# A routed mixture-of-experts round: the next tile is transposed two chunks sooner, its token numbers copied one round sooner

## The chip, the cores and the metric

The kernel runs on one core of a Trainium2 chip. The metric is the device time of one execution in microseconds (us). The engines are TensorE (PE; its weight loads are shown as PEld), VectorE (DVE), ScalarE (ACT), GpSimd (POOL) and SyncE (SP), which work side by side and wait for one another by semaphores. Transfers are issued by SP (direct ones, hardware queue) and by POOL (indirect ones with row numbers, software queue).

## What is computed

The reference is one block of gated cross-attention and one gated feed-forward block with two experts, on 8 x 256 tokens of 256 numbers, in float32. The part that the change touches is the second one, cut here to what matters:

```python
gate_scores = xf @ gate_w.T
top1 = jnp.argmax(gate_probs, axis=-1)
one_hot = jax.nn.one_hot(top1, N_ROUTING, dtype=xf.dtype)
masked = xf[None, :, :] * one_hot.T[:, :, None]
h = jax.nn.relu(jnp.einsum('end,edh->enh', masked, w1) + b1[:, None, :])
expert_out = jnp.einsum('enh,ehd->end', h, w2) + b2[:, None, :]
routing_output = expert_out.sum(axis=0)
shared = jax.nn.relu(xf @ sw1 + sb1) @ sw2 + sb2
return (routing_output + shared).reshape(B, S, D)
```

Every token thus gets a shared part, the part of its own expert (256 to 1024 hidden to 256), and for the other expert a constant row, since its input there is zero.

## The kernel before

**Stages.** Up to about 227 us the core works through attention and the shared part of the feed-forward block. Meanwhile each token's normalised row is scattered into `sorted_dram`, expert 0 from one end and expert 1 from the other, each row with its token number as a last column. The shared results lie in `part_dram`. Then come the routed rounds: 8 rounds of `RTOK` = 256 sorted rows, numbered 0 to 7 here, and behind them a half round for the 128 rows in which the experts meet. Each engine runs them in two loops, one per expert (`routed(j, e)`, loop variable `j`); in this run the first loop holds the earlier rounds and the second the later ones.

**Precision.** Each float32 operand is cut in two fp32r parts, hi and lo, and each product is three matmuls (`cut`). So ACT writes a hi part and the unrounded value, and DVE subtracts the two for the lo part.

**One round.** HIDDEN = 1024 is worked in 8 chunks of 128 (`HC`). I call the six matmuls that make chunk n's hidden values H_n (into `h_ps` or `s_ps`) and the six that add its share to the result Y_n (into `y_ps`). PE's order is H0 H1 H2 H3 Y0 H4 Y1 H5 Y2 H6 T Y3 H7 Y4 Y5 Y6 Y7: T is `sorted_turn(j + 1)`, four transposes of the next tile `xs` into one PSUM bank. ACT does for each chunk `hT_hi` and `h32` (lines 1083 and 1086), and behind chunk 6 `sorted_hi(j + 1)`, which copies the bank out (line 1018). DVE does for each chunk `hT_lo` (line 1469), which lets Y_n start, and besides:

- behind chunk 0, `gather_token` from the last column of `xs` (line 1475), once the tile has landed and the gathers of the round before are in; it raises `ids_copied`
- behind chunk 5, `scatter_token` from `gather_token` (line 1481), once the scatters of the round before have landed (`rows_out`)
- behind chunk 6, `sorted_lo(j + 1)` (line 1402), which needs `sorted_hi`
- behind Y7, `final` (line 1488), from `y_ps` and `part`; Y0 of the next round waits for it.

**Transfers of a round.** There is one buffer `xs`. SP loads the tile of round j + 1 into it once T of that buffer's last tile is done (`xsT_ps`) and its token numbers are out (`ids_copied`), and in rounds 0 to 3 it then copies a quarter of one expert's weights, 1 MB, into `sw` for the half round:

```python
def routed(j):
    sp.wait_ge(xsT_ps, j + 1)
    sp.wait_ge(ids_copied, j + 1)
    load_sorted(j + 1 - again)
```

POOL waits for `ids_copied` of the round and for `final` of the round before, issues two gathers from `part_dram` into `part` (line 807), waits for them, adds the other expert's row (line 814), and after `final` issues two scatters to `out` (line 821).

**What comes just ahead of round 0.** SP stores the last shared results (line 545), reads four numbers of the plan from SBUF into registers (lines 576 to 579), enters its loop and only then issues the load of tile 1. Tile 0 was loaded and transposed earlier, from the written-out orders.

Of the kernel before, what the change touches and what calls it, by code (L numbers as in the profile page):

```python
# [14 lines left out]
BATCHES, SEQ, DIM = 8, 256, 256  # L15
# [37 lines left out]
ROW = DIM + 1  # L53
# [23 lines left out]
LO_ON_POOL = (1, 4, 5)  # L77
FOLDED = {2, 4, 11, 12, 16, 19, 25, 29, 30, 31}
SORTED_BANK = 0
PE_ORDER = """  # L80
    warm.0 yt.0 yt.1 yt.2 yt.3 vt warm.1 kp.0.0 in.0.0 kp.0.1 kp.1.0 qy.0.1 kp.1.1 sc.0.0 vp.0 in.1.0 vp.1 vp.2
    qy.1.1 vp.3 sc.0.1 sc.0.2 sc.0.3 sc.1.0 sc.1.1 tn.0.0.0 tn.0.1.1 in.2.0 qy.2.1 sc.1.2 sc.1.3 tn.0.2.0
# [80 lines left out]
def build(nc, x, ctx_768, g_xattn, g_ffn, wq, bq, wk, bk, wv, bv, wo, bo,  # L163
# [13 lines left out]
    with ctx:  # L177
# [82 lines left out]
        xs = sb("xs", [P, RT, ROW])  # L260
# [587 lines left out]
        def _(act):  # L848
# [240 lines left out]
            def routed(j, e):  # L1089
                for c in range(HC):  # L1090
                    hidden(j, c, e)
                    if c == 6:
                        sorted_hi(j + 1, SORTED_BANK)

            with act.Fori(0, first) as j:
# [20 lines left out]
        def _(dve):  # L1116
# [282 lines left out]
            def sorted_lo(j, m):  # L1399

                dve.wait_ge(xsT_hi, j + 1)
                nc.vector.tensor_tensor(xsT[1][:, bass.ds(j % 2, 1), :, :].rearrange("p o k s -> p (o k s)"),
                                        bank[m][:, :],
                                        xsT[0][:, bass.ds(j % 2, 1), :, :].rearrange("p o k s -> p (o k s)"),
                                        ALU.subtract).then_inc(xsT_lo, 1)
# [4 lines left out]
            for step, at in walk(DVE_ORDER):  # L1410
# [47 lines left out]
                if step == "xsl":  # L1458
                    sorted_lo(0, *at)

            dve.wait_ge(seam_rdy, 1)
            first = dve.value_load(plan_int[0:1, FIRST:FIRST + 1], min_val=1, max_val=RTILES)
            rounds = dve.value_load(plan_int[0:1, ROUNDS:ROUNDS + 1], min_val=RTILES, max_val=MOST_ROUNDS)

            def routed(j, e):
                q = CHUNKS_SHARED + j * HC
                for c in range(HC):
                    dve.wait_ge(h_32, q + c + 1)
                    nc.vector.tensor_tensor(hT[1][:, c % HB, 0:RTOK], h32[:, c % 2, 0:RTOK], hT[0][:, c % HB, 0:RTOK],  # L1469
                                            ALU.subtract).then_inc(h_lo, 1)  # L1470
                    if c == 0:

                        dve.wait_ge(xs_in, 16 * (j + 1))
                        dve.wait_ge(gathered, 32 * j)
                        nc.vector.tensor_copy(gather_token[:, :], xs[:, :, DIM:ROW].rearrange("p t o -> p (t o)")
                                              ).then_inc(ids_copied, 1)
                    if c == 5:

                        dve.wait_ge(ids_copied, j + 1)
                        dve.wait_ge(rows_out, 32 * j)  # L1480
                        nc.vector.tensor_copy(scatter_token[:, :], gather_token[:, :]).then_inc(scatter_ids, 1)
                    if c == 6:
                        sorted_lo(j + 1, SORTED_BANK)

                dve.wait_ge(y_used, CHUNKS_SHARED + (j + 1) * HC)
                dve.wait_ge(part_rdy, RT * (j + 1))
                dve.wait_ge(rows_out, 32 * j)
                nc.vector.scalar_tensor_tensor(  # L1488
                    out=final[:, :, :].rearrange("p t d -> p (t d)"),
                    in0=y_ps[:, 0:RT, :].rearrange("p t d -> p (t d)"), scalar=gains[:, 1:2],  # L1490
                    in1=part[:, :, :].rearrange("p t d -> p (t d)"), op0=ALU.mult, op1=ALU.add
                ).then_inc(final_rdy, 1)
# [40 lines left out]
        def _(pe):  # L1533
# [293 lines left out]
            def routed(j, e):  # L1827
                q = CHUNKS_SHARED + j * HC
                pe.wait_ge(xsT_lo, j + 1)
                for n in range(HC + 3):  # L1830
                    if n < HC:

                        pe.wait_ge(h_32, q + n - 3)
                        for kc in range(KC):
                            ins = cut(hidden_bank(n % 4)[:, 0:RTOK],
                                      lambda m: ew1_sb[e][m][:, kc, n * P:(n + 1) * P],
                                      lambda m: xsT[m][:, bass.ds(j % 2, 1), kc, :].rearrange("p o s -> p (o s)"),
                                      kc == 0, kc == KC - 1)
                        ins.then_inc(h_in_ps, 1)
                    if n == 6:  # L1840
                        sorted_turn(j + 1, SORTED_BANK)
                    if n >= 3:
                        c = n - 3
                        pe.wait_ge(h_lo, LO_DVE + j * HC + c + 1)
                        if c == 0:
                            pe.wait_ge(y_out, len(UNITS))
                            pe.wait_ge(final_rdy, j)
                        for t in range(RT):
                            ins = cut(y_ps[:, t, :], lambda m: hT[m][:, c % HB, t * P:(t + 1) * P],
                                      lambda m: ew2_sb[e][m][:, c, :], c == 0 and t == 0, c == HC - 1,  # L1850
                                      skip_group_check=True)
                        ins.then_inc(y_used, 1)
# [51 lines left out]
```

## Time and profile before

| | us |
|---|---|
| median of 3 runs | 337.58 |
| lowest and highest | 336.97, 338.42 |
| span of the profiled execution | 339.1 |
| round 0 starts, half round starts (in the span) | 227.37, 325.42 |

The profile is one execution; its times count from the start of its span. A row of a timeline gives start, length, engine, line, operation, written and read tiles and a count of instructions in a row, and in brackets how long the engine was idle ahead of it and who ended that. The ends of matmuls are modelled, so their starts are the firmer numbers.

### The profile page before, as it was taken

To read this page: it belongs to the slowest core of one execution; us is meant where nothing else is said; L and a number is where in the kernel's file an instruction comes from. 1 tells how busy PE (TensorE), PEld (TensorE's weight loads), DVE (VectorE), ACT (ScalarE), POOL (GpSimd) and SP (SyncE) were. 2 spreads that over 40 slices of the span, in tenths; PEclk is the share of its full clock that TensorE was granted. 3 is DMA by queue.
4 is the path that set the end of the run, shared out by engine and by line. 5 is a ranking of instruction groups with operands and counts; after the bars stand their busy time and mean duration, and the time that the engine had idled before them with its cause. 6 is when DMAs were issued, how large, how long until landed. Compare 5 with 4: busy or idle time off the path is not lost.

```text
span 339.1 us, 7286 instructions
## 1 busy us (share of the span) xinstructions
PE 318.2 (94%) x2363; PEld 282.2 (83%) x2363; DVE 227.9 (67%) x516; ACT 215.6 (64%) x483; POOL 184.0 (54%) x261
## 2 busy tenths in 40 slices
PE   6997879899999999999999999999999999999993
PEld 5764666678988877788799889999999999999992
DVE  6999689999878899796767675534333544353463
ACT  2855898976786665658957584547546546464652
POOL 8226979885652564757371177432255536534542
PEclk9998599999999999999999999999999999999997
DMA  7992855274422030053160100315246233212300
GB/s 191 299 340 38 241 126 160 42 198 128 109 80 56 2 97 29 0 139 121 15 240 2 62 2 31 127 32 188 79 168 217 66 151 93 77 35 75 92 32 28
DMA packets 38150, 35.68 MB, mean 105 GB/s; under 512 B 16608, under 2 KB 35060, under 8 KB 37613
## 3 DMA queue, kind: packets, MB, share of 16 engines
q1 hardware_dynamic: 34568, 27.36, 28.5%
q0 software_dynamic: 2720, 7.32, 6.4%
q10 hardware_dynamic: 837, 0.67, 0.8%
q8 instruction: 14, 0.23, 0.3%
q14 instruction: 11, 0.09, 0.1%
HBM read 21.20 MB, written 9.85 MB: 92 GB/s over the span
## 4 chain that ended last, share of the span: by engine, by line
PE 61%; DVE 15%; ACT 8%; issue 7%; DMA 5%; POOL 1%; POOLq 1%; SPq 1%; DVEq 0%; ACTq 0%
PE y_ps L1535 20%; PE h_ps L1535 17%; PE bank L1535 9%; PE s_ps L1535 9%; DMA x_all<-in_x 5%; PE bank L1668 4%; ACT probs L947 2%; DVE rsum L1264 2%; DVE smax L1246 1%; DVE probs L1258 1%; DVE stats L1147 1%; DVE other_sum L1232 1%; ACT pT L956 1%; DVE hT_lo L1469 1%; ACT xn L898 1%
## 5 line engine op out<-in xcount | busy, mean ns | idle before, releaser
L690 POOL TENSOR_TENSOR probs<-probs,rinv 128x616 f32<-128x616 f32 x32 | 39.1, 1223 | 37.8 <-DVE rinv L1268 37.5
L1535 PE MATMUL y_ps<-sw,hT_hi 128*128 128x256 f32 x272 | 57.1, 290 | 1.2 <-DVE hT_lo L1513 1.2
L1535 PE MATMUL y_ps<-ew,hT_hi 128*128 128x256 f32 x256 | 54.1, 286 | 1.8 <-DVE hT_lo L1469 1.7
L1469 DVE TENSOR_TENSOR hT_lo<-h,hT_hi 128x256 fp32r<-128x256 f32 x64 | 29.2, 457 | 38.5 <-ACT h L1086 35.2
L1535 PEld LDWEIGHTS y_ps<-sw,hT_hi 128*128 128x128 f32 x272 | 44.9, 191 | 2.9 <-DVE hT_lo L1513 1.8
L1535 PEld LDWEIGHTS y_ps<-ew,hT_hi 128*128 128x128 f32 x256 | 42.4, 188 | 3.0 <-DVE hT_lo L1469 3.0
L1535 PE MATMUL h_ps<-x2T_hi,sw 128*128 128x512 f32 (+1 forms) x160 | 43.6, 359 | 0.1
L1083 ACT ACTIVATE hT_hi<-h_ps,vec_cols 128x256 fp32r<-128x256 f32 x32 | 15.2, 475 | 39.5 <-PE h_ps L1535 35.3
L995 ACT ACTIVATE hT_hi<-h_ps,vec_cols 128x512 fp32r<-128x512 f32 (+1 forms) x40 | 24.6, 614 | 21.9 <-PE h_ps L1535 17.3
L1535 PE MATMUL y_ps<-sw,hT_lo 128*128 128x256 f32 x136 | 38.4, 282 | 0.0
L1535 PE MATMUL y_ps<-ew,hT_lo 128*128 128x256 f32 x128 | 35.9, 280 | 0.0
L1264 DVE TENSOR_REDUCE rsum<-probs 128x8 f32<-128x616 f32 x32 | 25.1, 785 | 9.3 <-ACT probs L947 5.9
L821 POOL DMA_INDIRECT out<-final,scatter_token x16 | 18.0, 1127 | 24.6 <-DVE final L1488 19.2
L1535 PEld LDWEIGHTS h_ps<-x2T_hi,sw 128*128 128x128 f32 x160 | 26.8, 190 | 3.5 <-issue 0.8
L716 POOL TENSOR_TENSOR hT_lo<-h,hT_hi 128x512 fp32r<-128x512 f32 (+1 forms) x15 | 17.2, 1151 | 21.9 <-ACT h L1000 21.7
L1535 PE MATMUL h_ps<-x2T_lo,sw 128*128 128x512 f32 (+1 forms) x80 | 27.8, 348 | 0.0
L956 ACT ACTIVATE pT<-bank 128x512 f32<-128x512 f32 x40 | 23.7, 611 | 5.9 <-PE bank L1668 5.4
L1535 PE MATMUL h_ps<-xsT_parts,ew 128*128 x192 | 26.5, 280 | 0.0
L1535 PE MATMUL s_ps<-xsT_parts,ew 128*128 x192 | 26.4, 279 | 0.0
L1379 DVE TENSOR_TENSOR hT_lo<-h,hT_hi 128x512 fp32r<-128x512 f32 (+1 forms) x25 | 16.2, 654 | 15.0 <-ACT h L1000 15.0
L1535 PEld LDWEIGHTS y_ps<-sw,hT_lo 128*128 128x128 f32 x136 | 26.0, 191 | 0.2
L1668 PE MATMUL bank<-ident,probs 128*128 128x128 f32 (+1 forms) x160 | 24.3, 284 | 1.4 <-ACT pT L956 1.0
(206 smaller groups left out, 837.1 us busy)
## 6 DMA issues: line engine op xcount, KB each, us to landing
v_diag<-v_rows SPq DMA_DIRECT2D x16, 256.0 KB
stage<-in_L_ffn_w SPq DMA_DIRECT2D x4, 1024.0 KB, 5.6
sw<-ew SPq DMA_DIRECT2D x4, 1024.0 KB
xs<-sorted_dram SPq DMA_DIRECT2D x8, 257.0 KB
stage<-in_L_ffn_sw SPq DMA_DIRECT2D x2, 1024.0 KB, 6.6
x_all<-in_x SPq DMA_DIRECT2D x1, 1536.0 KB, 9.8
part_dram<-x_all SPq DMA_DIRECT2D x3, 512.0 KB, 2.9
k_dram<-probs SPq DMA_DIRECT2D x2, 616.0 KB, 5.9
```

The lines of the kernel that those rows point to most:

```text
L690: nc.gpsimd.tensor_tensor(pq, pq, rinv[:, b % 2, k, :].unsqueeze(2).to_broadcast([P, HG, KEYS]), ALU.mult).then_inc(p_ready, 1)
L716: nc.gpsimd.tensor_tensor(hT[1][:, q % HB, 0:width], h32[:, q % 2, 0:width], hT[0][:, q % HB, 0:width], ALU.subtract).then_inc(h_lo_pool, 1)
L821: pool.indirect_dma_start(out=out[:, :], out_offset=bass.IndirectOffsetOnAxis(ap=scatter_token[:, t:t + 1], axis=0), in_=final[:, t, :], i ...
L947: ins = nc.scalar.activation(to[:, h * KEYS:(h + 1) * KEYS], score_banks(quarter)[:, h // HH, keys], ACT.Exp, bias=smax[:, b % 2, k, h:h + 1])
L956: nc.scalar.activation(pT[:, 2 * u:2 * u + 2, :].rearrange("p c s -> p (c s)"), bank[m][:, :], ACT.Copy).then_inc(pT_sb, 1)
L995: nc.scalar.activation(hT[0][:, q % HB, 0:width], h_ps[:, q % 2, 0:width], ACT.Relu, bias=b1_sb[:, 0, c:c + 1]).then_inc(h_hi, 1)
L1083: nc.scalar.activation(hT[0][:, c % HB, 0:RTOK], hidden_bank(c % 4)[:, 0:RTOK], ACT.Relu, bias=b1_sb[:, 1 + e, c:c + 1]).then_inc(h_hi, 1)
L1264: nc.vector.tensor_reduce(out=rsum[:, b % 2, k, :], in_=probs[:, b % 2, k, :].rearrange("p (h k) -> p h k", k=KEYS), axis=AX_X, op=ALU.add ...
L1379: nc.vector.tensor_tensor(hT[1][:, q % HB, 0:width], h32[:, q % 2, 0:width], hT[0][:, q % HB, 0:width], ALU.subtract).then_inc(h_lo, 1)
L1469: nc.vector.tensor_tensor(hT[1][:, c % HB, 0:RTOK], h32[:, c % 2, 0:RTOK], hT[0][:, c % HB, 0:RTOK], ALU.subtract).then_inc(h_lo, 1)
L1535: return nc.tensor.matmul(out_, lhsT, rhs, start=start, stop=stop, **kw)
L1668: ins = nc.tensor.transpose(bank[m][0:ROWS[c], v * SEQ + t * P:v * SEQ + (t + 1) * P], probs[:, b % 2, g * TB + t, ROW0[c]:ROW0[c] + ROWS[ ...
```

## The change

T moves from behind H6 to behind H4 on PE, and with it `sorted_hi` on ACT and `sorted_lo` on DVE, from behind chunk 6 to behind chunk 4. The copy of the token numbers moves from behind chunk 0 of their own round to behind chunk 6 of the round before; the first copy stands ahead of DVE's loops. The count on `gathered` for which this copy waits grows by one round with it: it is now the gathers of the round in which it stands.

```diff
+TURN_AT = 4
@@ ACT
                 for c in range(HC):
                     hidden(j, c, e)
-                    if c == 6:
+                    if c == TURN_AT:
                         sorted_hi(j + 1, SORTED_BANK)
@@ DVE, ahead of the loops
+            def token_ids(j):
+
+                dve.wait_ge(xs_in, 16 * (j + 1))
+                dve.wait_ge(gathered, 32 * j)
+                nc.vector.tensor_copy(gather_token[:, :], xs[:, :, DIM:ROW].rearrange("p t o -> p (t o)")
+                                      ).then_inc(ids_copied, 1)
+
+            dve.wait_ge(xs_in, 16)
+            nc.vector.tensor_copy(gather_token[:, :], xs[:, :, DIM:ROW].rearrange("p t o -> p (t o)")
+                                  ).then_inc(ids_copied, 1)
@@ DVE, in a round
-                    if c == 0:
-
-                        dve.wait_ge(xs_in, 16 * (j + 1))
-                        dve.wait_ge(gathered, 32 * j)
-                        nc.vector.tensor_copy(gather_token[:, :], xs[:, :, DIM:ROW].rearrange("p t o -> p (t o)")
-                                              ).then_inc(ids_copied, 1)
+                    if c == TURN_AT:
+                        sorted_lo(j + 1, SORTED_BANK)
                     if c == 5:
 
                         dve.wait_ge(ids_copied, j + 1)
                         dve.wait_ge(rows_out, 32 * j)
                         nc.vector.tensor_copy(scatter_token[:, :], gather_token[:, :]).then_inc(scatter_ids, 1)
                     if c == 6:
-                        sorted_lo(j + 1, SORTED_BANK)
+                        dve.wait_ge(scatter_ids, j + 1)
+                        token_ids(j + 1)
@@ PE
-                    if n == 6:
+                    if n == TURN_AT:
                         sorted_turn(j + 1, SORTED_BANK)
```

On PE, in the first loop, the transposes before. They stand behind H6 (into `s_ps`), and the row after them is the start of Y3:

```order
L1535 MATMUL s_ps<-xsT_parts,ew 128x256 [waits h_32]
L1535 MATMUL s_ps<-xsT_parts,ew 128x256 x5
L1769 ISA
L1772 MATMUL bank<-ident,xs 128x128 [waits xs_in]
L1772 MATMUL bank<-ident,xs 128x128 x3
L1844 REGISTER_ALU
L1535 MATMUL y_ps<-ew,hT_hi 128x256 [waits h_lo]
```

And now, behind H4 (into `h_ps`) and ahead of Y1:

```order
L1543 MATMUL h_ps<-xsT_parts,ew 128x256 [waits h_32]
L1543 MATMUL h_ps<-xsT_parts,ew 128x256 x5
L1777 ISA
L1780 MATMUL bank<-ident,xs 128x128 [waits xs_in]
L1780 MATMUL bank<-ident,xs 128x128 x3
L1852 REGISTER_ALU
L1543 MATMUL y_ps<-ew,hT_hi 128x256 [waits h_lo]
```

What moved is the wait for `xs_in`: it now stands ahead of Y1, H5, Y2 and H6 too.

On DVE, in the first loop, the end of a round before, from the lo part of chunk 5 to that of chunk 7:

```order
L1469 TENSOR_TENSOR hT_lo<-h,hT_hi 128x256 [waits h_32]
L1481 COPY scatter_token<-gather_token 128x2 [waits rows_out,ids_copied]
L1468 REGISTER_ALU
L1469 TENSOR_TENSOR hT_lo<-h,hT_hi 128x256 [waits h_32]
L1401 REGISTER_ALU
L1402 ISA [waits xsT_hi]
L1402 REGISTER_ALU
L1402 TENSOR_TENSOR xsT_parts<-bank,xsT_parts 128x512
L1468 REGISTER_ALU
L1469 TENSOR_TENSOR hT_lo<-h,hT_hi 128x256 [waits h_32]
```

And now:

```order
L1480 TENSOR_TENSOR hT_lo<-h,hT_hi 128x256 [waits h_32]
L1487 REGISTER_ALU [waits ids_copied]
L1488 COPY scatter_token<-gather_token 128x2 [waits rows_out]
L1479 REGISTER_ALU
L1480 TENSOR_TENSOR hT_lo<-h,hT_hi 128x256 [waits h_32]
L1464 REGISTER_ALU [waits scatter_ids]
L1465 REGISTER_ALU [waits xs_in]
L1466 CAST gather_token<-xs 128x2 [waits gathered]
L1479 REGISTER_ALU
L1480 TENSOR_TENSOR hT_lo<-h,hT_hi 128x256 [waits h_32]
```

Between the lo parts of chunks 6 and 7 the subtraction of 128x512 is gone, and the small copy with its wait for `gathered` has come.

## Rows read from the trace of the kernel before

**Rows 1.** The page: busy time of the engines, and the group of DVE's lo parts.
```profile
PE 318.2 (94%) x2363; PEld 282.2 (83%) x2363; DVE 227.9 (67%) x516; ACT 215.6 (64%) x483; POOL 184.0 (54%) x261
...
L1469 DVE TENSOR_TENSOR hT_lo<-h,hT_hi 128x256 fp32r<-128x256 f32 x64 | 29.2, 457 | 38.5 <-ACT h L1086 35.2
```
**Rows 2.** Timeline of PE, H0 and H1 of rounds 0 to 4, 6 and 7, and of the half round.
```profile
227.37 1.56 PE L1535 MATMUL h_ps<-xsT_parts,ew 128*128 x12
...
239.68 1.58 PE L1535 MATMUL h_ps<-xsT_parts,ew 128*128 x12
...
252.85 1.64 PE L1535 MATMUL h_ps<-xsT_parts,ew 128*128 x12
...
265.51 1.58 PE L1535 MATMUL h_ps<-xsT_parts,ew 128*128 x12
...
277.57 1.58 PE L1535 MATMUL h_ps<-xsT_parts,ew 128*128 x12
...
301.09 1.59 PE L1535 MATMUL h_ps<-xsT_parts,ew 128*128 x12
...
313.63 1.60 PE L1535 MATMUL h_ps<-xsT_parts,ew 128*128 x12
...
325.42 1.11 PE L1535 MATMUL h_ps<-xsT_parts,sw 128*128 x8
```
**Rows 3.** Who waited for whom, 222 to 339.1 us: total, times, longest us.
```profile
DVE final L1488 <- POOL part L814: 4.8, 2, 3.5
...
DVE scatter_token L1481 <- DMA out<-final,scatter_token: 3.2, 2, 2.8
PEld y_ps L1535 <- DVE hT_lo L1469: 3.0, 6, 0.8
```
**Rows 4.** Timelines of SP (store, load, weight copy, load) and DVE (first token numbers).
```profile
228.35 0.36 SPq L545 DMA_DIRECT2D part_dram<-x_all  x1
232.01 0.42 SPq L549 DMA_DIRECT2D xs<-sorted_dram  x1
232.78 0.63 SPq L592 DMA_DIRECT2D sw<-ew  x1
243.29 0.39 SPq L549 DMA_DIRECT2D xs<-sorted_dram  x1
...
229.67 0.16 DVE L1475 CAST gather_token<-xs 128x2 uint32<-128x2 f32 x1
```
**Rows 5.** Timeline of PE in round 0: H4, start of Y1, H6, T.
```profile
230.88 0.86 PE L1535 MATMUL h_ps<-xsT_parts,ew 128*128 x6
231.58 0.28 PE L1535 MATMUL y_ps<-ew,hT_hi 128*128 128x256 f32 x1
...
233.70 0.86 PE L1535 MATMUL s_ps<-xsT_parts,ew 128*128 x6
234.93 0.66 PE L1772 MATMUL bank<-ident,xs 128*128 128x128 f32 x4 [0.37 <-DMA xs<-sorted_dram]
```
**Rows 6.** Timeline of PE and windows of PE (last: granted clock, DMA) at 28 to 44 us.
```profile
38.80 0.55 PE L1535 MATMUL bank<-xnT_hi,wqo_hi 128*128 128x256 f32 x1 [1.65 <-DVE xnT_lo L1239]
...
28.00:31.80 3.80, 1.95 (x7) 1.00 0.20 31
31.80:42.00 10.20, 7.96 (x38) 0.50 0.73 193
42.00:44.00 2.00, 1.94 (x20) 0.99 0.95 211
```
**Rows 7.** Timeline of POOL: the adds behind the gathers of rounds 0 and 3.
```profile
240.40 1.42 POOL L814 TENSOR_TENSOR part<-part,other_row 128x256 f32<-128x256 f32 x2 [4.97 <-DMA part<-part_dram,gather_token]
...
275.68 1.61 POOL L814 TENSOR_TENSOR part<-part,other_row 128x256 f32<-128x256 f32 x2 [2.88 <-DMA part<-part_dram,gather_token]
```
**Rows 8.** Timeline of DVE at the end of round 3: `sorted_lo`, then the lo part of chunk 7.
```profile
275.23 0.69 DVE L1402 TENSOR_TENSOR xsT_parts<-bank,xsT_parts 128x512 f32 x1 [0.23 <-ACT xsT_parts L1018]
275.84 0.86 DVE L1469 TENSOR_TENSOR hT_lo<-h,hT_hi 128x256 fp32r<-128x256 f32 x1
```

## The prediction, made before the changed kernel was run

> **What bounds the kernel now.** I read the page first: PE is busy 94% of the span [rows 1], so time can come only from the few places where PE stands still. In the routed rounds these are found by taking the starts of the rounds one from the next [rows 2]. Round 0 takes 239.68 - 227.37 = 12.31 us, round 1 13.17, round 2 12.66, round 3 12.06, rounds 4 and 5 together 301.09 - 277.57 = 23.52, or 11.76 each, round 6 12.54 and round 7 11.79. Every round has the same 96 matmuls and one T, so 11.76 is what PE needs for a round, and the rest is waiting: 0.55, 1.41, 0.90, 0.30, 0, 0, 0.78 and 0.03 us, together 3.97 us. That is all the change could ever win here.
>
> The waits by name [rows 3] say what it is, of the rounds and what lies around them. DVE copies `scatter_token` only when the scatters of the round before have landed, once 2.8 us late (round 1). The lo parts hold up PE's weight loads six times, 3.0 us in all. One example is round 3, where `sorted_lo` runs at 275.23 and the lo part of chunk 7 behind it, at 275.84, ends at 276.70 [rows 8]; Y7 would have been ready for it at about 276.4. `final` waited for POOL's adds 3.5 us in round 0, because the first gathers landed only at 240.40 [rows 7]. And T of round 0 waited 0.37 us for the load of tile 1 [rows 5].
>
> **Part 1: T behind H4, in rounds 1 to 7.** PE's work is only reordered: no instruction more. T needs tile j + 1 in `xs`, 2 x (H + Y) sooner than now. Its load is issued when `ids_copied` is raised, which also moves, from chunk 0 of the round to chunk 6 of the one before, some 3 us, so from round 1 on the load is in well before T: in round 1 the copy of the numbers can come as soon as the gathers of round 0 are in, 240.40, the load starts near 240.7 instead of 243.29 [rows 4], and T comes after 246. Price nothing. The cover is these 3 us; were it gone, T would wait in every round.
>
> What it wins: `sorted_lo`, 0.69 us, no longer stands between the lo parts of chunks 6 and 7, and on ACT `sorted_hi` no longer stands ahead of chunk 7. The rounds in which chunk 7's lo part was late are 2, 3 and 6: 0.90 + 0.30 + 0.78 = 1.98 us. Bounds are nothing and 1.98. What is late next is the new wait between the same two lo parts: `gather_token` needs the gathers of its own round. In round 3 they are in at 275.68 [rows 7], which is 10.17 us after the round's start at 265.51. With the small copy [rows 4], a lo part [rows 1] and some 0.1 us between them, 0.16 + 0.46 + 0.1, chunk 7 is ready at about 10.9; Y7's turn is at 11.76 - 0.71 = 11.05. So it fits, with 0.15 us to spare. I take -1.8 us, nearly all, because this landing is a late one, 2.88 us of waiting: in this round the 1 MB copy into `sw` is in flight with the gathers, and the copy now starts some 3 us sooner with the load ahead of it.
>
> **Part 2: T behind H4, in round 0.** This is the place where the change costs. The load of tile 1 is issued at 232.01, and not because of `ids_copied`: SP stores at 228.35 and then needs 3.7 us for the reads of its four registers and the entry of its loop [rows 4]; its wait on the numbers, which were out at 229.67 + 0.16 = 229.83, cost nothing. Copying the numbers sooner therefore does not bring this load forward. It lands in time for T at 234.93 [rows 5]. PE has done H4 by 231.58, when Y1 starts now. T will stand there, and PE with it, for 234.93 - 231.58 = 3.35 us. Now T follows H6, which would let it start at 233.70 + 0.71 = 234.41, so 0.52 of this is paid already. Round 0 gets longer by 3.35 - 0.52 = **2.83 us**; everything behind T in the round (Y1, H5, Y2, H6 and the rest) is queued behind it.
>
> **Part 3: round 1 hides what it waited for.** When PE arrives 2.83 us later, the things it waited for in round 1 are there: `final` of round 0 depends on the adds after 240.40, which do not move, and the scatters of round 0, whose landing held up `scatter_token`, start at most 1 us later than before. I let all of round 1's 1.41 us go: **-1.41**. The bound on the other side is nothing (the scatters move with PE). The new wait for `gathered` in round 0 ends at 240.40, and chunk 7's lo part would then be done at 241.1; in the new order Y7's turn comes at 242.51 - 0.71 = 241.8, so this hides too, with 0.7 us to spare.
>
> **Part 4: the clock.** PE has no standstill of 3.35 us anywhere in the trace; the longest is the 1.65 us ahead of 38.80. But the granted clock fell from 2.4 to 1.2 GHz (1.00 to 0.50) at 31.8, at the end of 3.8 us in which PE was busy for only 1.95 [rows 6]. The standstill in round 0 is emptier than that: 3.35 us of nothing. I expect the clock to fall there. It was back at 42.0, 3.2 us after the last gap's end at 38.80. In round 0 PE works without a gap behind T, so I take 3.2 us at half speed, which costs half of it, **+1.6 us**. The bounds: nothing, if the clock holds, and the whole 10.2 us from 31.8 to 42.0 at half, +5.1 us.
>
> The Trainium skill bears on this ("TensorE: Matmul & The Clock Gate", Part 1): the half rate is the default, and "activity releases the throttle". By that rule a PE that works densely behind the gap gets its clock back soon, and the sum would be near mine and not near +5.1; the trace shows the return only once, after a gap inside the slow stretch.
>
> **The sum.** +2.83 - 1.41 - 1.8 + 1.6 = +1.2 us. Against the profiled execution it is 339.1 + 1.2 = 340.3. That execution lies 1.5 us over the median of the runs, 337.58; the difference should carry over, so I forecast **338.8 us**, a little slower. Less than 0.5%, 1.7 us, is about what a measurement of this kernel can't tell from no change.
>
> The small copy ahead of the loops, 0.16 us on DVE, lies in its wait for the first `h32` of round 0; without that cover it would be 0.2 us. The half round's load comes sooner and nothing there waits for it.
>
> **Rivals.**
>
> *The clock holds.* For it: the gap is a single one, with dense work on both sides, and the fall in the trace came after two gaps. Then +2.83 - 1.41 - 1.8 = -0.4: 337.2 us.
>
> *The clock stays down longer*, up to the stretch of [rows 6]. Between +1.2 and 1.2 - 1.6 + 5.1 = +4.7; middle 340.5, slower. Against it: PE there had gaps inside the stretch.
>
> *The gather wait decides.* DVE stands in front of `gathered` between the lo parts of chunks 6 and 7, with chunk 7's lo part, and so Y7, behind it. It decides from the point where gathers land more than 10.3 us after the round's start. Round 3 has 10.17, and 4.97 us of waiting for the first gathers shows how late they can be when the weight copy goes ahead of them. If they land 0.6 us later in seven rounds, that is 7 x 0.4 = +2.8 on top: 341.6.
>
> *The late lo parts have another cause* than `sorted_lo` (ACT itself is late there), and rounds 2, 3 and 6 keep their waits: +1.2 + 1.8 = +3.0, 340.6.
>
> *The load is not late in round 0.* If SP did wait for the numbers after all and issued at 229 to 230, T would find its tile, only the wins would be left, about -1.8 and round 0's gather wait: 336.0 us. Against it stands the 3.7 us between SP's two issues.
>
> **How the numbers follow.** Chances: forecast 0.47, clock holds 0.24, clock down longer 0.12, gather wait 0.07, other cause of late lo parts 0.05, load not late 0.05. The range from 336.6 to 341.0 takes in the first two with their bounds on parts 1 and 3, and the middle of the next. Faster by over 0.5% (under 335.9) needs the last case or the second with luck: 0.08. Slower by over 0.5% (over 339.3): the three slower rivals and the upper fifth or so of the forecast, 0.33. Within: 0.59.
>
> **What the changed profile would show.** Part 2: T of round 0 with an idle time of about 3.3 us ahead of it, ended by the load of `xs`, and SP's load still 3.7 us behind its store. Part 4: a stretch of 0.50 in the granted clock between 235 and 240. Part 3: no wait of 2.8 us for `scatter_token` with PE behind it, round 1 at 11.8. Part 1: rounds 2 to 7 all near 11.8, and no PE wait on lo parts. I would be wrong if T of round 0 does not wait, or if the rows of waits name `gather_token` behind the gathers with PE idle after it.

## The result, and the profile after

| | kernel before | changed kernel |
|---|---|---|
| median | 337.62 us (22 runs) | 341.48 us (22 runs) |
| ratio, with its 95% interval | | 1.0106 [1.0079, 1.0134] |
| span of the profiled execution | 339.1 us | 340.7 us |
| time of the profiled execution | about 340.9 us | 342.54 us |
| rounds 0 to 7, start to start of the half round | 98.05 us | 99.98 us |
| what they take over 8 x 11.76 (waits, and the slow clock where it falls) | 3.97 us | 5.90 us |

The change makes the kernel 1.1% slower, 3.9 us by the medians and 3.6 by the ratio. The forecast was 338.8, in a range up to 341.0, so it missed. (One of the 22 runs, at 441.64 us, was disturbed and is left out of the ratio; without it the changed kernel's median is 340.97, since no run lies between 340.97 and 341.98 us.) The 340.9 of before is its span and the 1.84 us by which the changed kernel's time exceeds its span, 342.54 - 340.7.

First the starts of the routed rounds, read as in [rows 2]. The timeline of PE in the changed kernel, H0 and H1 of rounds 0, 1, 2 and 7 and the start of the half round:

```profile
227.09 1.56 PE L1543 MATMUL h_ps<-xsT_parts,ew 128*128 x12
...
244.83 1.57 PE L1543 MATMUL h_ps<-xsT_parts,ew 128*128 x12
...
256.55 1.62 PE L1543 MATMUL h_ps<-xsT_parts,ew 128*128 x12
...
315.33 1.56 PE L1543 MATMUL h_ps<-xsT_parts,ew 128*128 x12
...
327.07 1.12 PE L1543 MATMUL h_ps<-xsT_parts,sw 128*128 x8
```

Round 0 takes 244.83 - 227.09 = 17.74 us, where it took 12.31. Round 1 takes 11.72, and every later round lies between 11.72 and 11.80. So all that the change costs is in round 0, and every other round is at the floor.

In round 0 the changed kernel has T with its wait, on PE, and on SP the store, load and weight copy in the same places as in [rows 4]:

```profile
234.56 1.12 PE L1780 MATMUL bank<-ident,xs 128*128 128x128 f32 x4 [3.10 <-DMA xs<-sorted_dram]
...
228.07 0.36 SPq L546 DMA_DIRECT2D part_dram<-x_all  x1
231.74 0.42 SPq L550 DMA_DIRECT2D xs<-sorted_dram  x1
232.51 0.63 SPq L593 DMA_DIRECT2D sw<-ew  x1
```

PE stands for 3.10 us, against 0.37 in [rows 5]. SP's load is still 3.67 us behind its store, although the token numbers are now out long before. The four transposes take 1.12 us and not 0.66, which already tells of the clock. The windows of PE (start and end, length, busy time and instructions, granted clock, DMA share, GB/s), ahead of the standstill, in it, behind it, and behind that:

```profile
223.70:231.30 7.60, 7.60 (x65) 1.00 0.11 36
231.30:234.56 3.26, 0.16 (x2) 0.88 0.48 149
234.56:240.60 6.04, 6.04 (x29) 0.50 0.54 183
240.60:244.80 4.20, 4.20 (x37) 1.00 0.21 48
...
233.70:234.56 0.86, 0.00 (x0) 0.53 0.98 343
```

The granted clock is 1.00 (2.4 GHz), drops to 0.50 (1.2 GHz) before the standstill is over (0.53 already in the 0.86 us ahead of T, the last row), and stays there for 6.04 us of work in which PE has not a single gap: 29 instruction records where the same length at full clock holds some 50.

The waits, read as in [rows 3], 222 us to the end:

```profile
PEld bank L1780 <- DMA xs<-sorted_dram: 3.3, 1, 3.3
PE bank L1780 <- DMA xs<-sorted_dram: 3.1, 1, 3.1
...
PEld y_ps L1543 <- DVE hT_lo L1521: 1.8, 3, 0.8
...
DVE gather_token L1466 <- DMA part<-part_dram,gather_token: 0.2, 1, 0.2
```

`final` behind POOL's adds and `scatter_token` behind the scatters are gone from the list, and so are PE's waits for lo parts of the routed rounds; those that are left belong to the half round (line 1521). The new wait of `gather_token` is there once, with 0.2 us.

### The profile page after: what moved, and what is told of

The parts are those of the page before. It is cut to its first block, busy times and chain, and to the rows that moved or that the text cites. A ratio compares the mean times of both kernels' runs of the same rounds, so it can differ in the third digit from the quotient of the medians.

```text
span 340.7 us, 7287 instructions
## 1 busy us (share of the span) xinstructions
PE 319.1 (94%) x2363; PEld 284.0 (83%) x2363; DVE 231.1 (68%) x517; ACT 216.2 (63%) x483; POOL 182.9 (54%) x261
## 4 chain that ended last, share of the span: by engine, by line
PE 67%; DVE 13%; ACT 7%; DMA 5%; issue 4%; SPq 1%; POOL 1%; ACTq 0%; DVEq 0%; POOLq 0%
PE y_ps L1543 25%; PE h_ps L1543 18%; PE s_ps L1543 9%; PE bank L1543 8%; DMA x_all<-in_x 5%; PE bank L1676 4%; ACT probs L948 2%; DVE rsum L1265 2%; DVE smax L1247 1%; PE bank L1780 1%; ACT pT L957 1%; DVE probs L1259 1%; DVE stats L1148 1%; DVE other_sum L1233 1%; ACT xn L899 1%
## 5 line engine op out<-in xcount | busy, mean ns | idle before, releaser
L1480 DVE TENSOR_TENSOR hT_lo<-h,hT_hi 128x256 fp32r<-128x256 f32 x64 | 30.3, 473 | 37.6 <-ACT h L1087 37.6
L1543 PEld LDWEIGHTS y_ps<-ew,hT_hi 128*128 128x128 f32 x256 | 43.2, 193 | 0.0
```

What stands on the lines that cost most here:

```text
L1543: return nc.tensor.matmul(out_, lhsT, rhs, start=start, stop=stop, **kw)
```

## The experiments

Their names: a "standstill" is PE's idle time ahead of T in round 0. "Half speed" is a granted clock of 0.50. The round lengths are all read as above.

**How much of the waiting in [rows 2] is the kernel's own?** The kernel before, unaltered, was profiled a second time.

> The kernel before, unchanged, for a second profile. Theory: the profiled execution on which the prediction was built was a slow one (its span 339.1 would be a time of about 340.9, against a median of 337.6), and the waits of 3.97 us in its rounds were partly its own. Then another execution near the median shows well under 2 us of waiting over the eight rounds, that is 94.1 us plus less than 2. Rival: the waits are the same 3.97 us in every execution and the difference to the median lies ahead of the routed rounds; then the rounds again take 98 us.

Measured: 337.42 us, 1.0006 [0.9976, 1.0036], span 335.5, time of this execution 337.30. PE's timeline, H0 and H1 of rounds 0, 1 and 2 and the half round:

```profile
225.91 1.56 PE L1535 MATMUL h_ps<-xsT_parts,ew 128*128 x12
...
237.93 1.58 PE L1535 MATMUL h_ps<-xsT_parts,ew 128*128 x12
...
251.14 1.59 PE L1535 MATMUL h_ps<-xsT_parts,ew 128*128 x12
...
321.89 1.12 PE L1535 MATMUL h_ps<-xsT_parts,sw 128*128 x8
```

The rounds take 95.98 us, so their waits are 1.90 us and not 3.97. By round: 0.26, 1.45, 0.12, 0.13, and nothing from there on. Round 1's wait is the same in both executions. The waits of rounds 2, 3 and 6, which were 0.90, 0.30 and 0.78, are 0.12, 0.13 and 0.01. They belonged to that one execution. The traces show where they came from there. The first row is the start of Y1 in round 2 of the execution of [rows 2], so H4 was done at 257.13; then ACT's `hT_hi` of chunk 4 in that round, of chunk 5 in round 3 and of chunk 4 in round 6, and last that of chunk 4 in round 2 of the second execution:

```profile
257.13 0.28 PE L1535 MATMUL y_ps<-ew,hT_hi 128*128 128x256 f32 x1
...
258.62 0.47 ACT L1083 ACTIVATE hT_hi<-h_ps,vec_cols 128x256 fp32r<-128x256 f32 x1 [1.69 <-PE h_ps L1535]
...
272.75 0.47 ACT L1083 ACTIVATE hT_hi<-h_ps,vec_cols 128x256 fp32r<-128x256 f32 x1 [1.97 <-PE s_ps L1535]
...
307.36 0.47 ACT L1083 ACTIVATE hT_hi<-h_ps,vec_cols 128x256 fp32r<-128x256 f32 x1 [2.23 <-PE h_ps L1535]
...
255.58 0.47 ACT L1083 ACTIVATE hT_hi<-h_ps,vec_cols 128x256 fp32r<-128x256 f32 x1 [0.41 <-PE h_ps L1535]
```

ACT began chunk 4 of round 2 1.5 us after H4 was done, where the second execution needs 0.2 us (H4 done at 255.38), and every lo part behind it came late. In the first execution ACT was late like this in each of rounds 2 to 7 (in 4, 5 and 7 without holding PE up), in the second in none. Why ACT was late is not shown.

Round 0 starts 1.46 us sooner in the second execution, 225.91 against 227.37. The stretch of half speed of [rows 6], 10.2 us there, is 3.4 us long here:

```profile
37.70:41.10 3.40, 3.40 (x16) 0.50 1.04 305
```

**Is the late load the cause?** SP's register reads go ahead of its last store, in the changed kernel (twice) and in the kernel before (twice).

```diff
@@ SP
                 if step == "ps":
+                    if at[0] == len(UNITS) - 1:
+                        sp.wait_ge(seam_rdy, 1)
+                        sp.wait_ge(filled, 16)
+                        rounds = sp.value_load(plan_int[0:1, ROUNDS:ROUNDS + 1], min_val=RTILES, max_val=MOST_ROUNDS)
...
                     store_part(*at)
@@ behind the stages
-            sp.wait_ge(seam_rdy, 1)
-            sp.wait_ge(filled, 16)
-            rounds = sp.value_load(plan_int[0:1, ROUNDS:ROUNDS + 1], min_val=RTILES, max_val=MOST_ROUNDS)
...
```

The other three reads, shown as "...", move with the first.

> The changed kernel, but SP reads its four registers ahead of its last store and not behind it, so that the load of tile 1 is issued right behind the store (about 228.5 instead of 231.74) and lands before H4 is done. Theory (standstill plus clock in round 0 are the whole loss): the 3.1 us of standstill and the 2.8 us of half clock go, and 5.9 us less than the changed kernel would be 335.6; but PE then reaches the end of round 0 before the first gathers are in (240.8), so I expect 1 to 1.5 us of waiting for the copy of the token numbers and 336.5 to 337.5 us, a ratio to before of 0.997 to 1.001. Rival (the new order costs something in every round): the rounds stay longer than 11.76 us and the time stays at 340 or more.

> The kernel before with SP's register reads ahead of its last store, as in e1. It tells whether the new order is worth anything once its standstill is gone. Theory: the weight copy of round 0 is out of the way of the first gathers here too, so the waits of rounds 0 and 1 shrink, and what is left for the new order is only the late lo parts, under 0.5 us: 336 to 337 us, ratio 0.994 to 0.999, and within 0.3% of e1. Rival (the early transposes are worth the 2 us that the prediction gave them): e1 is over 1.5 us faster than this.

> The changed kernel with SP's four register reads ahead of its last store, a second time, beside the kernel before with the same edit. In their profiles both had no waits left in the routed rounds (sums 0.26 and -0.11 us), so by the theory that the change has nothing more to win once the load of tile 1 is early, both have the same time within 0.3%, near 336 to 337, ratio 0.994 to 0.998. Rival: the new order itself costs something that the profiled execution didn't show (T's wait in round 0 with the load 1.4 us after the store): then this one is slower than its twin by 1 to 1.5 us, at ratio 0.998 to 1.000.

> The kernel before with SP's four register reads ahead of its last store, a second time and on the same chip as its twin with the change. If the first look (335.88, ratio 0.993) holds: ratio 0.991 to 0.996, and no PE wait over 0.3 us in rounds 0 to 7. If that look owed something to its chip, the ratio is 0.997 to 1.000.

| | first time | second time, both on one chip |
|---|---|---|
| changed kernel | 337.33, 0.9985 [0.9954, 1.0017] | 336.90, 0.9992 [0.9962, 1.0023] |
| kernel before | 335.88, 0.9931 [0.9896, 0.9966] | 336.54, 0.9974 [0.9949, 1.0000] |

The changed kernel with this edit, on SP and PE:

```profile
228.41 0.37 SPq L546 DMA_DIRECT2D part_dram<-x_all  x1
229.38 0.41 SPq L550 DMA_DIRECT2D xs<-sorted_dram  x1
...
232.02 0.66 PE L1780 MATMUL bank<-ident,xs 128*128 128x128 f32 x4 [0.22 <-DMA xs<-sorted_dram]
```

The load comes 0.97 us behind the store instead of 3.67, the standstill is 0.22 us (0.41 the second time), round 0 takes 12.14 us, and the time falls by 4.2 us against the changed kernel's first median. The edit brings two transfers forward, the load and the weight copy behind it, and with the copy early the first gathers land sooner too (last section). So the whole loss hangs on what SP issues late ahead of round 0; the standstill by itself is tested at the end. The edit is also the version to keep, without the change. The kernel before with it (second time), H0 of round 0 and of the half round:

```profile
226.27 1.56 PE L1535 MATMUL h_ps<-xsT_parts,ew 128*128 x12
...
320.24 1.11 PE L1535 MATMUL h_ps<-xsT_parts,sw 128*128 x8
```

Eight rounds in 93.97 us are 11.75 each, no wait at all. It was 0.7% faster in one comparison and 0.3% in the other, whose interval just reaches 1. The second set was run on another chip to see whether the first owed something to its chip, and leaves that open. With the edit the new order has nothing left to win, and by the second pair, 336.90 and 336.54, little to lose (rounds of 94.80 and 93.97 us in the profiled executions).

**T alone, in all rounds.** T behind H4; the token numbers copied behind chunk 0, as before. The edit stands on ACT and DVE, and as `n == 4` on PE.

```diff
-                    if c == 6:
+                    if c == 4:
                         sorted_hi(j + 1, SORTED_BANK)
```

> One half of the change alone: T stands behind H4, but the token numbers are copied behind chunk 0 of their own round, as before. By the prediction's step on the cover: the next tile's load is issued about 3.6 us after a round's start (before: 243.29 - 239.68), a load took 2.9 us to its end there (232.01 to 234.93), so the tile is in 6.5 us after the start, while T's turn comes 4.2 us after it (231.58 - 227.37). If the sooner copy is what covers T, T waits some 2 us in each of rounds 1 to 7, less where DVE's copy comes early in the round, and the rounds have 12.5 to 14 us: 8 to 14 us over before, ratio 1.02 to 1.04. The rival, that PE's move alone made no wait except in round 0 and the sooner copy is needless: rounds 1 to 7 at 11.8, time as the changed kernel's, 341.5, ratio 1.010. Round 0 should show the same 3.1 us standstill either way, since its load is late behind SP's register reads.

Measured: 350.05 us (4 runs), 1.036 [1.0294, 1.0426]. PE's timeline, T of rounds 0, 1 and 2 and H0 of round 2, and SP's load in round 2:

```profile
234.30 0.66 PE L1772 MATMUL bank<-ident,xs 128*128 128x128 f32 x4 [3.23 <-DMA xs<-sorted_dram]
...
249.05 0.66 PE L1772 MATMUL bank<-ident,xs 128*128 128x128 f32 x4 [1.30 <-DMA xs<-sorted_dram]
...
262.31 0.66 PE L1772 MATMUL bank<-ident,xs 128*128 128x128 f32 x4 [1.34 <-DMA xs<-sorted_dram]
...
256.60 1.57 PE L1535 MATMUL h_ps<-xsT_parts,ew 128*128 x12
...
259.23 0.40 SPq L549 DMA_DIRECT2D xs<-sorted_dram  x1
```

T waits in all eight rounds. In rounds 1 to 6 it is 1.2 to 1.34 us, less than the 2 us that I had expected, since the load is issued 2.63 us behind the round's start at 256.60 and not 3.6. The prediction's cover is real: without the sooner copy the move costs in every round.

**The token numbers alone.** The changed kernel with `TURN_AT = 6`.

> The changed kernel with the transposes back behind the seventh chunk: the half of the change that copies the token numbers out a round sooner, alone. Theory: no standstill in round 0 beyond some 0.3 us, no fall of the clock; the copy waits in round 0 for the first gathers (about 240.6), which puts about 1 us on PE in place of the wait before final; rounds 1 to 7 at 11.8 or a little more. 337.5 to 338.8 us, ratio 1.000 to 1.004. Rival (the wait for the gathers between the lo parts of chunks 6 and 7 is what costs): 340 or more, with PE waits on lo parts in several rounds.

Measured: 341.55 us (6 runs), 1.0119 [1.0071, 1.0166], as slow as the whole change. That is the time of the expectation's rival, but with a wait in round 0 only. PE with its longest idle time, DVE just before it, and the windows of PE around it:

```profile
241.68 0.58 PE L1543 MATMUL y_ps<-ew,hT_hi 128*128 128x256 f32 x1 [2.19 <-DVE hT_lo L1480]
...
240.58 0.17 DVE L1466 CAST gather_token<-xs 128x2 uint32<-128x2 f32 x1 [2.79 <-DMA part<-part_dram,gather_token]
240.68 0.95 DVE L1480 TENSOR_TENSOR hT_lo<-h,hT_hi 128x256 fp32r<-128x256 f32 x1
...
239.50:241.60 2.10, 0.00 (x0) 1.00 0.00 0
241.60:245.00 3.40, 3.32 (x15) 0.51 0.86 287
245.00:250.00 5.00, 5.00 (x44) 0.99 0.40 142
```

This is the prediction's rival "the gather wait decides", in round 0 alone. DVE stands for 2.79 us in front of `gathered`, with chunk 7's lo part behind it, and PE 2.19 us in front of Y7. Round 0 takes 15.22 us. Then the clock falls here too, for 3.4 us. Not all of the 4.1 us is this: the rounds of this execution take 98.32 us, 2.3 more than in the second execution of the kernel before, and another 2.0 us lie ahead of round 0, which starts at 227.91, though PE's work there is unchanged. In the whole change the wait for the gathers is hidden by the standstill ahead of it, and PE pays for the first wait that it meets.

**Where T stands in round 0.** Once `TURN_AT = 5` in all rounds, and once 6 in round 0 and 4 in all others (round 0 written out ahead of the loops of PE, ACT and DVE).

```diff
+            routed(0, 0, FIRST_TURN_AT)
-            with pe.Fori(0, first) as j:
+            with pe.Fori(1, first) as j:
                 routed(j, 0)
```

> The changed kernel with TURN_AT = 5, T behind H5, one H and one Y later than in the change. Theory: the standstill in round 0 is 1.41 us shorter, about 1.7 us. If the clock holds at that, round 0 takes 13.2 to 13.7 us and the time is 338 to 339; if it falls, about 1.7 us more, 340. Either way the round's length is 11.76 plus the standstill plus what the clock takes. Rival (order of the later rounds costs): the same 341.5 as the change.

> The changed kernel with round 0 written out ahead of the loops, and in round 0 alone the transposes behind the seventh chunk; rounds 1 to 7 as in the change. Theory: the loss sits in round 0 only, so this gives it back: no standstill, no fall of the clock, 337 to 338.5 us, ratio 0.998 to 1.003, rounds 1 to 7 at 11.76. Rival (the order of rounds 1 to 7 costs): 340 or more.

Measured: with 5, 338.41 us, 1.0002 [0.9972, 1.0032]; with 6 in round 0, 337.03 us, 0.9994 [0.9963, 1.0025]. At 5, T waits less and the gathers take over; both idle times of PE in round 0:

```profile
233.65 0.66 PE L1780 MATMUL bank<-ident,xs 128*128 128x128 f32 x4 [1.77 <-DMA xs<-sorted_dram]
...
240.52 0.39 PE L1543 MATMUL y_ps<-ew,hT_hi 128*128 128x256 f32 x1 [1.25 <-DVE hT_lo L1480]
```

Round 0 takes 15.23 us, where 13.2 to 13.7 was expected if the clock holds: the expectation had left out the gathers. Its clock held, and all ten runs are at 339.13 us or below, above which 29 of the changed kernel's 32 lie (its two sets of runs). With 6 in round 0 the longest idle time is 0.78 us (Y7 again), rounds 0 and 1 wait 2.6 us together, and the time is that of the kernel before.

**The clock.** The changed kernel was profiled again; it was also run with round 0 written out and nothing else changed, twice; and that form with matmuls in the standstill, twice.

```diff
                     if n == turn_at:
+                        if isinstance(j, int):
+                            for _ in range(14):
+                                mm(bank[1][:, 0:P], ident[:, :], ident[:, :], True, True)
                         sorted_turn(j + 1, SORTED_BANK)
```

> The changed kernel, unaltered, to see what its standstill does to the clock in another execution and how its times are spread. Theory: the wait for tile 1 (3.1 us) is there in every execution and costs 3.4 us, and the clock falls behind it in some executions and holds in others; so the times lie in two groups, near 340 with a mean granted clock of 0.986 or more and near 343 with 0.976 to 0.982. Rival: the clock falls every time and the spread has its cause before the routed rounds; then the mean clock does not separate the two groups. Ratio 1.008 to 1.013 by both.

> The changed kernel with round 0 written out ahead of the loops and nothing else: the control for the next run. Expected as the changed kernel: T of round 0 stands 2.5 to 3.2 us, the clock falls to 0.5 for 3.4 to 7 us, rounds 1 to 7 at 11.76, 340 to 342 us. If the writing out itself matters, T waits for a clearly different time.

> The run before plus 14 matmuls of the identity with itself ahead of T in round 0, into a PSUM bank that nothing reads any more; they fill the standstill, which stays as long as it was. Theory (the standstill costs twice, once by itself and once through the clock): the clock stays at 1.00 through round 0, which gets 1.7 to 2.9 us shorter than in the control, 14.8 to 15.2 us by its length; 338 to 339.5 us. Rival (the fall of the clock is harmless, since PE then waits for others anyway): same time as the control.

> The changed kernel with round 0 written out ahead of the loops of PE, ACT and DVE and otherwise the same, as the twin of the run with the extra matmuls. Expected by the theory: a group of 3 to 6 of some 12 runs near 342 with a mean clock of 0.983 or less, the others near 339, ratio 1.005 to 1.010. By the rival the same, but with the group in the twin too.

> The written-out form with 14 matmuls of the identity into the second PSUM bank ahead of T in round 0 (work that the reference has not, its result unused), a second time. Theory (the group near 342 us is the fall of the clock behind the standstill): PE has no standstill, no run lies near 342 with a mean clock of 0.983 or less, median 338.5 to 339.5, ratio 1.003 to 1.005, and the highest group is gone. Rival (the group comes from elsewhere, such as the start or the transfers): the group stays, about as many runs as in the form without the extra work.

| | median us | ratio | round 0 | at half speed around T |
|---|---|---|---|---|
| changed kernel | 341.48 | 1.0106 [1.0079, 1.0134] | 17.74 | 6.8 |
| again | 340.50 | 1.0090 [1.0057, 1.0123] | 16.43 | 3.4 |
| written out | 339.62 | 1.0062 [1.0025, 1.0099] | 15.27 | none |
| written out, again | 341.25 | 1.0084 [1.0048, 1.0120] | 17.73 | 6.8 |
| with matmuls | 339.50 | 1.0047 [1.0015, 1.0078] | 15.18 | none |
| with matmuls, again | 338.97 | 1.0033 [1.0004, 1.0063] | 15.06 | none |

The last two columns are those of the one profiled execution of each. The same standstill, 3.01 to 3.15 us, came with 6.8 us at half speed, with 3.4 or with none. T in the written-out form, its first profile and its second (the transposes' own length tells the clock), and then the matmuls and T of the form that has them:

```profile
232.80 0.66 PE L1783 MATMUL bank<-ident,xs 128*128 128x128 f32 x4 [3.01 <-DMA xs<-sorted_dram]
...
234.10 1.11 PE L1783 MATMUL bank<-ident,xs 128*128 128x128 f32 x4 [3.03 <-DMA xs<-sorted_dram]
...
230.07 3.29 PE L1547 MATMUL bank<-ident 128*128 128x128 f32 x28
233.34 0.66 PE L1784 MATMUL bank<-ident,xs 128*128 128x128 f32 x4
```

What it costs is then plain: 17.73 - 15.27 = 2.5 us for 6.8 us at half speed, 16.43 - 15.27 = 1.2 for 3.4. The 15.27 holds about 0.3 us in which Y7 waits for chunk 7's lo part, behind the gathers, and the slow clock covers this wait in the others; so the clock by itself costs nearer 2.8 and 1.4 us.

How often it happens must be read from the runs' mean granted clocks, and these count the whole execution, the stretch of [rows 6] too. A low mean alone proves nothing of round 0: with SP's reads early, 7 of 48 runs have 0.981 or less, and six of them take 336.73 to 337.99 us; and the execution profiled in the next experiment has 3.4 us at half speed in round 0 at a mean of 0.993. So the two forms have to be compared. In the second comparison the form with a standstill has six of twelve runs at a mean of 0.981 or less, and they are its six slowest, 341.60 to 342.59 us; the other six take 338.67 to 340.90. The form with matmuls has none under 0.986 and none over 340.82. Of the 29 runs of the kernel before beside them none has 0.981 or less. In the first comparison four of ten runs against none had the low clock, though the medians, 339.62 and 339.50, hardly differ. Over both, 10 of 22 runs with a standstill have a mean of 0.982 or less, and none of 22 with the matmuls. That tells the two theories apart: a group near 342 comes from the clock, and it goes when PE works through the wait, though T starts no sooner for it.

The clock doesn't explain every long time. One run with the matmuls took 342.37 us at 0.992. The changed kernel's first set has 342.82 and 343.60 us at 0.991. In its second set the five runs at 0.982 or less (340.34 to 341.93) overlap with the other six (338.67 to 341.00). With SP's reads early (first time), where the standstill is 0.22 us, two of twelve runs took 341.10 and 341.51. Their cause is open.

What decides whether the clock falls is open too. The form alone doesn't decide it: the changed kernel showed 6.8 and 3.4 us, the written-out form none and 6.8.

**The standstill alone.** The kernel before with round 0 written out and T behind H4 in that round only.

> The kernel before with round 0 written out and T behind H4 in that round alone; everything else, the copy of the token numbers too, as before. T waits 3.0 to 3.3 us and round 0 has 15.2 us. If the step on round 1 holds, the waits of rounds 1 and 2 (1.2 to 2.3 us in the two looks at the kernel before) go, and the time is +1.5 us, or +1.5 to +4 with the clock: ratio 1.004 to 1.010, the same as the whole change. The rival, that the waits of the later rounds are independent of PE's arrival, leaves them: +3 us or more without the clock, ratio 1.010 to 1.016.

Measured: 340.68 us, 1.0085 [1.0047, 1.0123]. H0 and H1 of rounds 0, 1 and 2 on PE, and T in round 0:

```profile
225.32 1.56 PE L1539 MATMUL h_ps<-xsT_parts,ew 128*128 128x256 f32 x12
...
241.97 1.56 PE L1539 MATMUL h_ps<-xsT_parts,ew 128*128 x12
...
253.74 1.60 PE L1539 MATMUL h_ps<-xsT_parts,ew 128*128 x12
...
232.86 0.66 PE L1776 MATMUL bank<-ident,xs 128*128 128x128 f32 x4 [3.17 <-DMA xs<-sorted_dram]
```

Round 0 takes 16.65 us (3.4 us at half speed), round 1 11.77: its wait is gone with nothing changed but PE's arrival. T moved in one round of eight costs about what the whole change costs.

## Why the prediction was wrong, point by point

Parts 2 to 4 had the mechanism right; Part 4 had its size too small. What failed most is the base and, with it, Part 1. Measured against the second execution of the kernel before, whose time is that of the median, the terms are these:

| step | forecast | measured | from |
|---|---|---|---|
| Part 1, lo parts of rounds 2, 3, 6 | -1.8 | -0.3 | waits 0.12 + 0.13 + 0.01 |
| Part 2, standstill in round 0 | +2.83 | +3.25 | 15.27 - 12.02 |
| Part 3, round 1 | -1.41 | -1.49 | 13.21 to 11.72 |
| Part 4, clock, where it falls for 6.8 us | +1.6 | +2.5 | 17.73 - 15.27 |
| sum | +1.2 | +4.0 | medians: +3.9 |

That the sum meets the medians is partly luck: it holds for executions in which the clock falls for 6.8 us, and the second set of runs is 340.50 - 337.68 = 2.8 us slower than the kernel before beside it.

**The base, the step that failed first.** "That execution lies 1.5 us over the median ... the difference should carry over." It set a span against a median of times. Its own time was about 340.9, so it lay 3.3 us over the median, near the slowest of 22 runs, 341.74. A long time has its reasons. Here 2.07 us of it were the very waits that the change removes, 3.97 us where the second execution has 1.90, and 1.46 us lay ahead of round 0. Neither profiled execution of the changed kernel has these waits: rounds 1 to 7 take 82.24 and 82.31 us, and 7 x 11.76 is 82.32. The first came to 340.7, only 0.4 from the 340.3 that the sum gave. So against the execution before, in which Part 1's waits were there to be won, the sum was nearly right, with 0.28 us of luck from an earlier start of round 0. The difference to the median was what did not carry over.

**Part 1** failed with it: 0.3 us to win where it took 1.8, so the lower bound, nothing, was nearer. It blamed `sorted_lo` between the lo parts. But the second execution has `sorted_lo` in the same place and waits 0.12 and 0.13 us in rounds 2 and 3. What made rounds 2, 3 and 6 late in the execution of [rows 2] was ACT, which began chunks 4 or 5 some 1.5 to 2 us late (the rows in the first experiment). It could have been suspected, since rounds 4, 5 and 7 run the same instructions in the same order without that wait. Whether the new order would hide such lateness isn't shown, since ACT was late like this in no profiled execution of the changed kernel outside the slow clock.

**Part 2** was right in all it said: T waited 3.10 us for the load, SP's load stayed 3.67 us behind its store, and the sooner numbers did not bring it forward. The term was 0.4 short. Round 0 of the kernel before had 0.55 us of waits to give back in that execution and has 0.26 in the second, and the 15.27 holds about 0.3 us of Y7's wait behind the gathers; the standstill itself was a little shorter than forecast.

**Part 3** was right, and the standstill alone gives it by itself (round 1 in 11.77 us).

**Part 4** had the mechanism and not the size. I took 3.2 us of half speed from the last gap's end to the clock's return in [rows 6]; it was 6.8 us here, 3.4 in other executions, none in others. The Trainium skill ("TensorE: Matmul & The Clock Gate", Part 1: "activity releases the throttle") gave me the reason to take a short return. The trace agrees that the clock comes back while PE works densely, but after a time that the row of before did not show. For the price, the Trainium skill ("TensorE: Matmul & The Clock Gate", "Terms") has the penalty as the time at the lower clock times the share of the clock that is missing. That share is half here, and the estimate by it 3.4 us for 6.8. The rounds show 2.5, and the rounds decide. Two things make the difference: the half-speed stretch begins inside the standstill, where it costs nothing (0.86 us of it lie ahead of T), and it covers the 0.3 us of Y7's wait.

**The rivals.** "The clock stays down longer" is what happened in the changed kernel's first profiled execution, and it had 0.12. Its middle, 340.5, is 1.0 us short. "The gather wait decides", at 341.6, comes nearest by its number, but by luck: it was priced for seven rounds, and `gather_token` waited once, for 0.2 us, in each of the changed kernel's two profiled executions. In round 0 it stood in line behind the standstill; with the numbers alone moved it cost 2.2 us there, and in the written-out form, whose clock held, about 0.3 us in round 0 and 0.47 in round 2. So my estimate for round 0, 0.7 us to spare, did not hold either. "The clock holds" happened too, for certain in the first profiled execution of the written-out form (338.95 us). It gives 339, not the 337.2 that it was priced at from the same base. "The late lo parts have another cause", with "ACT itself is late there", had 0.05 and named the cause; what it did not see is that the lateness was that of one execution, so no round kept its wait. "The load is not late" is what the edit on SP makes true; it gives 336.9 to 337.3, against 336.0 forecast.

## What to carry to other kernels

Before a wait is counted as a gain, look whether a second execution of the same kernel has it, and set times against times: a profiled execution that lies over the median can carry waits that the median hasn't, as this one did. When an instruction that waits for a transfer is moved forward, the first pass through the loop needs its own sum, since there the transfer's issue hangs on what stands ahead of the loop; here the place of four register reads decided over 1%, and moving them in the kernel before paid 0.3 to 0.7%, more than any new order. A standstill of PE of 2 to 3 us cost its length here, and in many executions the clock's fall on top.

## What the runs showed of the hardware

- The granted clock fell to 0.50 around single standstills of 2.19 to 3.23 us with dense work on both sides, but in some executions only, for 3.4 or 6.8 us. With two idle times of 1.77 and 1.25 us in a round its profiled execution held it. With matmuls whose result is unused, 3.29 us of them in the wait, it stayed up in both profiled executions.
- Indirect gathers issued right behind a 1 MB copy landed later than those issued some 3 us after it, but by a varying amount. POOL's adds in round 0 of the changed kernel (two executions), with the copy issued 0.27 and 0.28 us ahead of the first gather, and of the same kernel with SP's reads early, where it is 3.25 us:

```profile
240.78 1.43 POOL L815 TENSOR_TENSOR part<-part,other_row 128x256 f32<-128x256 f32 x2 [5.61 <-DMA part<-part_dram,gather_token]
...
238.57 1.61 POOL L815 TENSOR_TENSOR part<-part,other_row 128x256 f32<-128x256 f32 x2 [3.34 <-DMA part<-part_dram,gather_token]
...
237.60 1.61 POOL L815 TENSOR_TENSOR part<-part,other_row 128x256 f32<-128x256 f32 x2 [1.83 <-DMA part<-part_dram,gather_token]
```

The wait behind the gathers' issue, in brackets, is 5.61 and 3.34 us in the one form and 1.83 in the other (1.82 in its second execution).

- The start of round 0, ahead of which nothing was changed on PE, lies between 225.19 and 227.91 us in the 17 profiled executions. That is a spread of 2.7 us, against 3.9 for the whole change. It goes mostly with the half-speed stretches between 31 and 44 us: executions without one start at 225.19, 225.32, 225.41 and 226.69, six with 3.4 us of it at 225.85 to 226.46, six with 6.8 us at 226.69 to 227.91, and the one of [rows 6], with 10.2 us, at 227.37.
